# Opening of a one-core attention kernel: products of zeros on TensorE, and another order of the first transfers

## The reference, cut to what matters

```
def _layernorm(x, axis=-1, eps=1e-05):
    m = jnp.mean(x, axis=axis, keepdims=True)
    v = jnp.var(x, axis=axis, keepdims=True)
    return (x - m) / jnp.sqrt(v + eps)
...
q = query @ Wq.T + bq
k = mem_state @ Wk.T + bk
v = mem_state @ Wv.T + bv
scores = jnp.einsum('btd,bsd->bts', q, k) * scale
...
alpha = jax.nn.softplus(wave_damping)[:, None]
omega = wave_frequency[:, None]
phi = wave_phase[:, None]
kernels = jnp.exp(-alpha * t[None, :]) * jnp.cos(omega * t[None, :] + phi)
coupling = jax.nn.softmax(field_coupling, axis=-1)
...
x = x + _L0_xattn_ref(_layernorm(x, axis=-1), ctx_1024, 32, ...)
x = x + _L0_attn_ref(_layernorm(x, axis=-1), ...)
x = x + _L0_ffn_ref(_layernorm(x, axis=-1), ...)
```

## Time and profile before

| what | value |
|---|---|
| median of 3 runs | 459.78 us (457.98 to 460.98) |
| the profiled execution, reported time | 461.32 us |
| its span, first to last instruction | 459.5 us |
| TensorE busy | 439.7 us, 96% |
| VectorE busy | 299.3 us, 65% |
| ScalarE busy | 215.7 us, 47% |
| GpSimd busy | 127.2 us, 28% |
| granted TensorE clock, mean | 0.993 |
| chain that ended last | PE 71%, DVE 13%, ACT 6%, DMA 5% |

### The profile page before, as it was taken

One profiled execution on the slowest core, in us unless ns is written; L12 is line 12 of the kernel. 1 busy time (PEld: TensorE's weight loads), 2 busy tenths in 40 slices (PEclk: granted clock), 3 DMA queues, 4 the chain that ended last, 5 costly groups with the idle time before them and its releaser, 6 DMA issues.

```text
span 459.5 us, 5828 instructions
## 1 busy us (share of the span) xinstructions
PE 439.7 (96%) x2045; PEld 325.5 (71%) x2045; DVE 299.3 (65%) x591; ACT 215.7 (47%) x321; POOL 127.2 (28%) x195
## 2 busy tenths in 40 slices
PE   6999999799999999898999999999999999999996
PEld 2587766356567656576888888887788888888884
DVE  3898787688999999968997443646862333522224
ACT  1797764354566454384877446434542111111111
POOL 3501013032222330200003272324236643333330
PEclk9999999799999999999999999999999999999999
DMA  6999924044224314103951700000000000200002
GB/s 207 412 391 386 366 98 180 2 183 183 74 112 183 139 45 184 35 11 141 396 198 38 168 1 23 1 0 1 1 1 1 1 0 1 86 7 0 1 0 92
DMA packets 26845, 49.98 MB, mean 109 GB/s; under 512 B 6208, under 2 KB 6208, under 8 KB 25792
## 3 DMA queue, kind: packets, MB, share of 16 engines
q1 hardware_dynamic: 26816, 49.61, 30.2%
HBM read 47.49 MB, written 2.11 MB: 108 GB/s over the span
## 4 chain that ended last, share of the span: by engine, by line
PE 71%; DVE 13%; ACT 6%; DMA 5%; issue 3%; SPq 1%; POOL 0%; DVEq 0%; ACTq 0%
PE bank L1237 8%; PE bank L1239 8%; PE bank L1238 8%; PE bank L1447 7%; PE bank L1678 7%; PE bank L1676 6%; PE bank L1662 6%; PE bank L1663 6%; PE bank L1418 5%; PE bank L1344 3%; DMA wab<-w1T 2%; PE bank L1244 2%; DVE mt_lo L1026 2%; PE bank L1432 2%; DVE work L1039 2%
## 5 line engine op out<-in xcount | busy, mean ns | idle before, releaser
L792 ACT ACTIVATE g<-bank,b1c 128x512 f32<-128x512 f32 x32 | 22.0, 688 | 92.0 <-PE bank L1678 92.0
L1217 DVE CAST g_hi<-g 128x512 fp32r<-128x512 f32 x32 | 13.9, 436 | 74.7 <-ACT g L792 74.6
L594 ACT ACTIVATE mt_hi<-bank 128x512 fp32r<-128x512 f32 x64 | 38.0, 600 | 49.4 <-PE bank L1418 49.4
L1026 DVE TENSOR_TENSOR mt_lo<-bank,mt_hi 128x512 fp32r<-128x512 f32 x64 | 43.1, 684 | 18.1 <-ACT mt_hi L594 17.9
L1676 PE MATMUL bank<-xt_lo,w1s 128*128 128x512 f32 x128 | 50.8, 397 | 0.0
L1678 PE MATMUL bank<-xt_hi,w1s 128*128 128x512 f32 x128 | 50.7, 396 | 0.0
L1662 PE MATMUL bank<-w2s,g_lo 128*128 128x512 f32 x128 | 50.3, 393 | 0.2 <-DVE g_lo L1219 0.2
L1663 PE MATMUL bank<-w2s,g_hi 128*128 128x512 f32 x128 | 50.0, 390 | 0.0
L487 POOL TENSOR_SCALAR w2s<-w2t 128x512 fp32r<-128x512 int8 x32 | 19.8, 620 | 65.9 <-PE bank L1663 65.9
L445 POOL TENSOR_SCALAR qs<-qT 128x256 fp32r<-128x256 f32 x16 | 6.5, 405 | 112.8 <-PE bank L1433 93.5
L1432 PE MATMUL bank<-mt_lo,qs 128*128 128x512 f32 x64 | 30.6, 479 | 0.3 <-DVE mt_lo L1026 0.3
(11 more groups left out here) (244 smaller groups left out, 1101.0 us busy)
## 6 DMA issues: line engine op xcount, KB each, us to landing
ctxr<-ctx SPq DMA_DIRECT2D x8, 1024.0 KB, 8.5
ctx<-ctx SPq DMA_DIRECT2D x8, 1024.0 KB, 7.7
wab<-w1T SPq DMA_DIRECT2D x4, 1024.0 KB, 11.4
wab<-w2T SPq DMA_DIRECT2D x4, 1024.0 KB, 8.5
wgraw<-wgT SPq DMA_DIRECT2D x4, 1024.0 KB, 6.5
wst<-w1T SPq DMA_DIRECT2D x4, 1024.0 KB, 6.2
wst<-w2T SPq DMA_DIRECT2D x4, 1024.0 KB, 6.6
resid<-x SPq DMA_DIRECT2D x4, 512.0 KB, 6.8
```

The source lines that it names most:

```text
L594: act.activation(mt_hi[:, g % 4, :], ctx_bank(g)[:, :], ACT.Copy).then_inc(mt_hi_ok, 1)
L1026: dve.tensor_tensor(mt_lo[:, g % 4, :], ctx_bank(g)[:, :], f(mt_hi[:, g % 4, :]), ALU.subtract).then_inc(mt_lo_ok, 1)
```

## The change

Three things. TensorE gets seven products of a 128x128 tile of zeros (`mix_hi`, which is written with its real content much later) into bank 7, ahead of the first step of `m1`. GpSimd zeroes that tile first of all, which makes five counts of `consts` where there were four, and all waits for 4 become waits for 5. SyncE issues the second wq and wk ahead of the first x, the third ahead of the second x, the fourth ahead of the third; `phase` and `coup` go from before the first x to behind the second one. The programs of VectorE and ScalarE are the same but for the count of `consts`.

```diff
@@ -296,15 +296,13 @@
         @block.sync
         def _(sp):
 
-            def first_loads(o):
+            def first_weights(o):
 
                 sp.dma_start(wqraw[:, o, :], rows(wq)[:, o, :]).then_inc(wqk_in[o], 16)
                 sp.dma_start(wkraw[:, o, :], rows(wk)[:, o, :]).then_inc(wqk_in[o], 16)
-                if o == 0:
-                    sp.dma_start(cols[:, :, :], small[0]).then_inc(small_in, 16)
-                    for n, a in enumerate((freq, damp, phase)):
-                        sp.dma_start(wpar[:, n, :], a.partition_broadcast(P)).then_inc(par_in, 16)
-                    sp.dma_start(cpl[0:H, :], coup).then_inc(par_in, 16)
+
+            def x_load(o):
+
                 sp.dma_start(resid[:, 2 * o:2 * o + 2, :], x_v[:, 2 * o:2 * o + 2, :]).then_inc(x_in[o], 16)
 
             def abs_load(k):
@@ -317,8 +315,19 @@
 
                 sp.dma_start(w_place(k, wst[:, k % 4, :]), w_chunk(k)).then_inc(wst_in[k % 4], 16)
 
-            for o in range(DC):
-                first_loads(o)
+            first_weights(0)
+            sp.dma_start(cols[:, :, :], small[0]).then_inc(small_in, 16)
+            sp.dma_start(wpar[:, 0, :], freq.partition_broadcast(P)).then_inc(par_in, 16)
+            sp.dma_start(wpar[:, 1, :], damp.partition_broadcast(P)).then_inc(par_in, 16)
+            first_weights(1)
+            x_load(0)
+            first_weights(2)
+            x_load(1)
+            sp.dma_start(wpar[:, 2, :], phase.partition_broadcast(P)).then_inc(par_in, 16)
+            sp.dma_start(cpl[0:H, :], coup).then_inc(par_in, 16)
+            first_weights(3)
+            x_load(2)
+            x_load(3)
             for k in range(3):
                 abs_load(k)
             sp.dma_start(woraw[:, :, :], rows(woT)).then_inc(wo_in, 16)
@@ -387,6 +396,7 @@
                 pool.wait_ge(pool_step, steps[0])
 
 
+            pool.memset(f(mix_hi[:, :]), 0.0).then_inc(consts, 1)
             link(pool.memset(ident[:, :], 0.0))
             pool.affine_select(out=ident[:, :], in_=ident[:, :], compare_op=ALU.not_equal, fill=1.0, base=0,
                                pattern=[[-1, P]], channel_multiplier=1).then_inc(consts, 1)
@@ -394,7 +404,7 @@
             pool.memset(half_pi[:, :], TWO_PI / 4).then_inc(consts, 1)
             pool.memset(ones[:, :], 1.0).then_inc(consts, 1)
 
-            pool.wait_ge(consts, 4)
+            pool.wait_ge(consts, 5)
             pool.memset(lag_none[:, :], 0.0).then_inc(tpos_ok, 1)
             pool.iota(tpos[:, 0:NC], pattern=[[P, NC]], base=0, channel_multiplier=1,
                       allow_small_or_imprecise_dtypes=True).then_inc(tpos_ok, 1)
@@ -568,7 +578,7 @@
             act.wait_ge(dec_ok, 1)
             act.activation(tdec[:, :, :], tdec[:, :, :], ACT.Exp, scale=-1.0).then_inc(cos_ok, 1)
             act.wait_ge(arg_ok, 1)
-            act.wait_ge(consts, 4)
+            act.wait_ge(consts, 5)
             act.activation(targ[:, :, :], targ[:, :, :], ACT.Sin, bias=half_pi[:, :], scale=-1.0).then_inc(cos_ok, 1)
             abs_part(4)
             q_part(4)
@@ -904,7 +914,7 @@
             link(dve.tensor_scalar(cpl[0:H, :], cpl[0:H, :], rinv[0:H, 0:1], None, ALU.mult))
             dve.tensor_copy(cpr[0:H, :].rearrange("p (h e) -> p h e", e=E8),
                             cpl[0:H, :].unsqueeze(2).to_broadcast([H, H, E8])).then_inc(cpr_ok, 1)
-            dve.wait_ge(consts, 4)
+            dve.wait_ge(consts, 5)
             dve.tensor_reduce(mask8[:, :], ident[:, :].rearrange("p (h e) -> p e h", e=E8), AX.X,
                               ALU.add).then_inc(cpr_ok, 1)
 
@@ -1261,9 +1271,12 @@
                     pe.wait_ge(xt_lo_ok, t - 1)
                 turn(turn_bank(t), first_xn(t)).then_inc(xn_turned, 1)
 
+            pe.wait_ge(consts, 1)
+            for n in range(7):
+                pe.matmul(bank[7][:, 0:P], f(mix_hi[:, :]), f(mix_hi[:, :]), start=True, stop=True)
             for o in range(DC - 1):
                 m1_step(o)
-            pe.wait_ge(consts, 4)
+            pe.wait_ge(consts, 5)
             for t in range(4):
                 turn_first(t)
             m1_step(DC - 1)
```

## The result

| | before | after |
|---|---|---|
| median of the runs | 459.03 us (4 runs, 457.98 to 460.98) | 464.55 us (4 runs, 463.87 to 465.81) |
| ratio | | 1.0119, 95% interval 1.0074 to 1.0163 |
| profiled execution, reported / span | 461.32 / 459.5 us | 465.81 / 464.0 us |

The changed kernel is 5.5 us slower by the medians. That is +1.2%, past the 1% line that the text drew (the 28% case), and inside the stated range. The interval begins at 0.7%, so slower is shown, and slower by over 1% is likely and not certain.

What follows compares the result with a forecast made beforehand. TensorE, busy 96% of the span, bounds the body; in the opening VectorE's rigid statistics block gates it. Statistics 3.8 us late, less 0.9 slack, is 2.9; with half clock 3.7: 459.8 + 3.7 = 463.5 us, range 460.0 to 466.0.

Steps and rivals of the forecast that it cites:

- the 28% case: Whole kernel: slower than before by over 1%, beyond 464.4 us; chance 28%, against 69% within 1% and 3% faster.
- The zeros: TensorE's opening: seven products from about 1.0 to 4.0-4.3 us cost nothing; earlier fast clock takes 1.7 us off.
- The swallowing: TensorE before the last `m1` step: the clock's 1.7 us are swallowed whole by the wait for turned tiles.
- The order of landing: Opening transfers: one queue lands them in issue order, so `phase` and `coup` come behind the second x.
- rival C: Tables not held up, `nmax` starts by 8.0, `q` products at most 0.9 us earlier; 458.9 to 459.8 us; 12%.
- The landing time: Opening queue: all four tables there at 11.9 us (11.6 to 13.1) instead of 7.65: 5.78 + 8 x 0.68, plus 0.7.
- my upper bound: Opening queue: what the two tables themselves add to the landing, at most 1.9 us, as in the opening before.
- the lower one: Opening queue: the two tables add only 0.4 us, from the full queue at 55 us; 0.7 taken, near it.
- The rigid block: VectorE's eight layer statistics: a delayed begin delays the end equally; 3.8 us later (3.5 to 5.0).
- The 0.9 us of slack: Between `m_lo`'s first quarter near 23.5 and the first `q` product at 24.47; cuts the 3.8 us shift to 2.9.
- The half clock: TensorE's last `m1` step: the gap drops the clock to 1.2 GHz; shift 3.0 to 4.7 us, 3.7 taken.
- Reaching the end: After the first `q` product: the shift is TensorE's own and nothing gives it back; 3.7 us reach the end.

Runs made afterwards that it cites:

- zeros alone: Kernel before with only the seven products of zeros added on TensorE; ratio 1.002 (0.9998 to 1.0043), 10 runs.
- `coup` alone late: Changed kernel with `phase` put back right behind `damp`, only `coup` behind the second x; ratio 1.0105 against before (1.0078 to 1.0133).
- readers moved: Changed kernel, transfers and zeros kept, with the instructions that read the four tables moved behind the statistics; ratio 1.0057 against before (1.0035 to 1.0078).
- `phase` alone late: Changed kernel with `coup` put back right behind `damp`, only `phase` behind the second x; ratio 1.0137 against before (1.0105 to 1.0169).
- tables last: Changed kernel with table readers moved behind the statistics and all four tables issued behind the last x; ratio 1.0074 against before (1.0047 to 1.01).
- transfers alone: Changed kernel without the products of zeros, only the new order of transfers; ratio 1.0147 against before (1.0117 to 1.0177).
- tables in front: Changed kernel with `phase` and `coup` issued right behind `damp` again, all else kept; ratio 1.0023 against before (0.9999 to 1.0047).
- only the tables late: Kernel before with only `phase` and `coup` moved behind the second x; ratio 1.0086 (1.007 to 1.0101).
- readers moved in the kernel before: Kernel before, transfers untouched, with the readers of the four tables moved behind the statistics; ratio 1.0008 (0.9987 to 1.0028).
- more zeros: Changed kernel with further products of zeros before the turns: ten before the first, four before each other; ratio 1.0147 against before (1.0103 to 1.0191).
- the kernel with the eleven products added: The kernel with the tables last plus eleven products of `ident` in TensorE's wait near 83 us; ratio 1.0052 against before (1.0032 to 1.0072).
- the wait filled: Kernel before with eleven products of `ident` in TensorE's wait near 83 us; ratio 0.9989 (0.9974 to 1.0004), 12 runs.

## Why the prediction was right, and where it was off

- *The zeros* were costed rightly: 0.99 to 4.3 us, nothing on the path. The three steps took 1.7 us less, as said (13.29 to 11.55), but only 1.03 of it is theirs against the same transfers without them (12.58).
- *The swallowing* held: with zeros alone the 1.7 us did not reach the end, and in the changed kernel TensorE waited 2.54 us at the first turn.
- *The order of landing* held for the table that decides. `coup`, the last of the four, landed at 6.83 + 7.35 = 14.2, behind the second x. It did not hold in full: `phase` landed at 6.17 + 5.7 = 11.9, 0.6 us ahead of the second x (12.5), which was requested ahead of it. That agrees with the sentence of the Trainium skill (DMA: Bandwidth & Descriptors, "Queues, rings and completion order") that completion is not first-in-first-out for one engine's requests. The overtaking was by 0.6 us and not by the 4 that rival C needed, and `nmax` waits for the last of the four, so rival C did not come.
- *The landing time* of that last table was mis-sized, in two terms of the sum. The kernel after, SyncE's issues, then us to landing of `phase` and of the second x:

```profile
5.47 0.66 SPq L306 DMA_DIRECT2D resid<-x  x1
...
6.17 0.62 SPq L326 DMA_DIRECT2D wpar<-phase  x1
...
6.83 0.44 SPq L327 DMA_DIRECT2D cpl<-coup  x1
...
wpar<-phase SPq DMA_DIRECT2D x1, 8.0 KB, 5.7
...
resid<-x SPq DMA_DIRECT2D x1, 512.0 KB, 7.0
```

  The second x landed at 5.47 + 7.0 = 12.5, where 5.78 + 8 x 0.68 had given 11.2: it came 1.3 us later than the mean rate says. And `coup` came 14.2 - 12.5 = 1.7 behind it, near my upper bound (1.9, from the opening) and not near the lower one (0.4, from the full queue at 55 us), which I chose because the queue would be full. In the other kernels with a late table the last one came 0.1 to 2.0 us behind the second x (`coup` alone late: 6.64 + 6.2 against 5.94 + 6.8; readers moved: 6.57 + 6.8 against 5.47 + 5.9), so neither bound by itself would have been safe. 11.9 became 14.2, outside my 11.6 to 13.1. Part of that is this execution: with the same order of transfers `nmax` began at 13.53 and 12.83 in two other kernels. But all three are later than 11.9.
- *The rigid block* held exactly: 6.20 us in, 6.19 out.
- *The 0.9 us of slack* before the first `q` product was real, and 0.8 in size (6.2 became 5.87 - 0.43 = 5.4 without the clock).
- *The half clock* fell where it was said to, and its price was 0.43 us, not the 0.8 that lay between 2.9 and 3.7. That error and the landing's had opposite signs at this step.
- *Reaching the end* held up to the scores' product. Behind it, the clock's second fall differs from execution to execution, and this pair differed by 1.4 us in favour of the changed kernel.

So the mechanism was right, and the size was inside the range because its bounds were wide: the landing ran 2.3 us over the likeliest value, past its own upper bound. The likeliest shift, 3.7, was 5.5 by the medians; the baseline's own median moved down by 0.75 with one run more, and so, by luck, the absolute time came out nearer (464.55 against 463.5) than the shift did. The ratio belongs to the slower case that got 28%: the landing was the term that decided it.

## What to carry to other kernels

A small transfer is cheap to move for the one who moves, and dear for whoever stands behind its wait: before moving a request back in a queue, look for the first instruction in each engine's program that waits for it, and at what stands behind that instruction. A time gained on the engine that is busiest is worth nothing while its next input comes from another engine's fixed block; find the gate, then its second gate, before counting. For the landing of a small transfer behind large ones, don't take one row: here rows of the same program gave 0.4 and 1.9 us, the runs 0.1 to 2.0. Keep the wide bound, and let the likeliest value lie between the rows. A wait that a new order opens on the busy engine can cost twice, once as the wait and once as the clock behind it.

## What the runs showed of the hardware that I had not expected

- In a filling queue a table of 1 KB that stood behind 2 MB landed 1.7 us after the second x; one table late cost about as much as two (`nmax` at 14.28 with `phase` alone, 12.99 with `coup` alone, 12.83 and 14.28 with both in two kernels). The `phase` table of 8 KB, requested between the two, landed at 11.9, ahead of both (12.5 and 14.2).
- Where small tables stood behind large transfers, the rate of the whole queue fell in some executions: 90 GB/s for half a microsecond in the changed kernel, 71 GB/s over 2 us with all four tables last, against some 400 otherwise. Why is open.
- With the same instructions in the same place, the half clock behind the wait near 83 us lasted 6.8 us in the trace of before, some 3.4 in five others (the changed kernel, zeros alone, transfers alone, readers moved, tables last), and did not come in six (tables in front, `phase` alone late, `coup` alone late, only the tables late, readers moved in the kernel before, more zeros), although TensorE waited 2.8 us in each. With the wait filled, none of twelve runs had a mean clock below 0.998. Between the groups of before's runs it moves the time by 0 to about 3 us. The wait of 3.02 us at 53 in the kernel with the tables last was followed by 6.8 us of half clock; the wait of 1.67 in the same place, in the kernel with the eleven products added, by none.
- Products of zeros raised the clock as others do: in the nine traces with them the weight loads of `m1` came at the fast pace from 4.7 to 6.7 us on, in the five without them from 8.4 to 10.4 on.
